# Mamba, attention and expert blocks on one core: expert weights split once and reloaded, shorter maximum and gate, and another order of steps between recurrences

## The reference

```
1  h = rmsnorm(x);  xi, z = split(h @ in_proj);  xi = silu(conv4(xi))
   dt, B, C = split(xi @ x_proj);  delta = softplus(dt @ dt_proj + b)
   s_t = s_(t-1) * exp(delta_t * A) + delta_t * B_t * xi_t        (16 states)
   y_t = sum_n s_t[n] * C_t[n];  x = ln(2x + ((y + D xi) * silu(z)) @ out_proj)
2  q with rotary positions, 8 heads, 128 keys of a fixed context
   x = ln(x + relu(ln(x + softmax(q k / sqrt(32)) v @ W_o) @ W_ffn))
3  top-2 of 8 experts by softmax(x @ gate), and one shared expert:
   x = ln(x + sum_e c_e * (silu(x @ w1_e + b1) * (x @ w3_e + b3)) @ w2_e)
```

## Time and profile before

| | |
|---|---|
| median of 3 runs | 1169.25 us (1169.08 to 1170.02) |
| the profiled execution | 1168.82 us, its span 1167.0 us |
| PE busy | 916.1 us (79%) |
| DVE busy | 828.9 us (71%) |
| ACT busy | 545.8 us (47%) |
| POOL busy | 535.4 us (46%) |
| granted TensorE clock, mean | 0.861 |
| DMA per expert besides w13s | w2s 256 KB, weight row (cbc) 256 KB; B (bbc) 512 KB for 4 steps |
| first recurrence (chunk 0 alone) | 61.8 to 160 us |
| recurrences of chunks 1, 2, 3 begin | 215.28, 478.05, 740.8 us |
| drain | from about 943 us |

### The profile page before, as it was taken

One profiled execution on the slowest core, in us unless ns is written; L12 is line 12 of the kernel. 1 busy time (PEld: TensorE's weight loads), 2 busy tenths in 40 slices (PEclk: granted clock), 3 DMA queues, 4 the chain that ended last, 5 costly groups with the idle time before them and its releaser, 6 DMA issues.

```text
span 1167.0 us, 13071 instructions
## 1 busy us (share of the span) xinstructions
PE 916.1 (79%) x4208; PEld 697.8 (60%) x4208; DVE 828.9 (71%) x1222; ACT 545.8 (47%) x1015; POOL 535.4 (46%) x318
## 2 busy tenths in 40 slices
PE   4857688486788998486788998477789985767996
PEld 2446673265677883265677883265678872645885
DVE  1699964698999954698999954698999961213233
ACT  3556736453455526453455526453555512413342
POOL 1267710743468720743468720743468723001552
PEclk9979999796689999796689999796689996755998
DMA  5111102101033302101033302102033212001330
GB/s 202 38 36 55 37 1 74 54 19 64 28 104 114 92 10 92 54 19 64 28 102 112 95 10 92 54 19 64 28 100 103 88 36 91 0 1 37 102 123 29
DMA packets 37714, 71.96 MB, mean 62 GB/s; under 512 B 3856, under 2 KB 12185, under 8 KB 37647
## 3 DMA queue, kind: packets, MB, share of 16 engines
q1 hardware_dynamic: 37646, 71.13, 18.9%
HBM read 64.62 MB, written 2.30 MB: 57 GB/s over the span
## 4 chain that ended last, share of the span: by engine, by line
PE 28%; issue 20%; POOL 19%; DVE 13%; ACT 5%; POOLq 0%; DMA 0%; DVEq 0%; ACTq 0%; SPq 0%
POOL dbu L537 11%; PE ps L928 8%; PE ps L1005 5%; DVE hs L1111 3%; POOL work L572 3%; PE ps L902 3%; PE ps L759 2%; DVE yacc L1164 2%; PE ps L848 2%; POOL w_lo L564 2%; DVE mx L1260 2%; POOL work L558 2%; POOL work L554 2%; PE ps L842 1%; ACT work L707 1%
## 5 line engine op out<-in xcount | busy, mean ns | idle before, releaser
L537 POOL TENSOR_TENSOR dbu<-v,bbc 128x1024 f32<-128x1024 f32 x128 | 301.8, 2364 | 218.0 <-DVE v L1097 124.4
L1111 DVE TENSOR_TENSOR_SCAN hs<-ps,carry,dbu 128x512 f32<-128x512 f32 x256 | 312.9, 1265 | 0.6 <-PE ps L759 0.6
L645 ACT ACTIVATE ps<-delta,neg_a 128x512 f32<-128x512 f32 x256 | 175.2, 691 | 174.0 <-DVE hs L1111 174.0
L759 PE MATMUL ps<-ident,hs 128*128 128x128 f32 x1024 | 161.2, 303 | 65.9 <-DVE yacc L1164 47.5
L759 PEld LDWEIGHTS ps<-ident,hs 128*128 128x128 f32 x1024 | 133.8, 158 | 90.5 <-DVE hs L1111 64.1
L564 POOL TENSOR_TENSOR w_lo<-w13s,w_hi 128x512 fp32r<-128x512 f32 x72 | 93.4, 1297 | 130.4 <-ACT w_hi L734 129.2
L1164 DVE SCALAR_TENSOR_TENSOR yacc<-ps,ctok,yacc 128x512 f32<-128x512 f32 x210 | 147.3, 737 | 1.9 <-PE ps L759 1.0
L1005 PE MATMUL ps<-w2s,work 128*128 128x256 f32 x576 | 136.3, 380 | 0.3
L747 ACT ACTIVATE work<-ps,half_b 128x512 f32<-128x512 f32 x72 | 49.6, 689 | 143.8 <-PE ps L928 139.8
L1005 PEld LDWEIGHTS ps<-w2s,work 128*128 128x128 f32 x576 | 105.8, 190 | 14.9 <-DVE work L1282 1.5
L928 PE MATMUL ps<-x_hi,w_hi 128*128 128x512 f32 x288 | 108.4, 458 | 7.6 <-DVE work L1282 7.3
(11 more groups left out here) (169 smaller groups left out, 1322.4 us busy)
## 6 DMA issues: line engine op xcount, KB each, us to landing
w13s<-in_w SPq DMA_DIRECT2D x72, 256.0 KB, 2.9
bbc<-brow_dram SPq DMA_DIRECT2D x32, 512.0 KB, 4.0
w2s<-in_w SPq DMA_DIRECT2D x36, 256.0 KB, 2.7
cbc<-comb_dram SPq DMA_DIRECT2D x32, 256.0 KB, 3.5
work<-work SPq DMA_DIRECT2D x16, 256.0 KB, 2.3
xn<-in_x SPq DMA_DIRECT2D x4, 512.0 KB, 4.7
xt<-in_x SPq DMA_DIRECT2D x4, 512.0 KB, 4.8
rope<-in_rope_q SPq DMA_DIRECT2D x4, 512.0 KB, 5.4
```

Source lines behind the costliest of these rows:

```text
L537: pool.tensor_tensor(dbu[:, i % DRING, :, :], v[:, 2 * h:2 * h + 2, :], bbc[:, n // 2 % 2, n % 2, :].rearrange("p (o t) -> p o t", o=1) .t ...
L645: act.activation(ps[:, unit % 2, :], delta[:, q, :], ACT.Exp, scale=neg_a[:, q * NS + m:q * NS + m + 1]).then_inc(da_done.sem, 1)
L759: last = pe.transpose(ps[:, bank, t * P:(t + 1) * P], src(t), ident[:, :])
L1111: dve.tensor_tensor_scan(hs[:, m % 2, q, 0:TC], ps[:, unit % 2, :], dbu[:, n % DRING, q % 2, :], carry[:, m, q:q + 1], ALU.mult, ALU.add). ...
```

## The change

It does four things.

1. **Weights split once.** During the recurrence of chunk 0 each of the 18 halves is loaded raw, split on ACT and POOL, and both parts are stored to DRAM (new step "split", at s = 2 to 20). Each chunk then loads both parts, twice 256 KB a half, into a ring of 4. The raw buffers share memory with xa and x2.
2. **Maximum.** 1/sqrt(32) is multiplied into the keys at set-up, DVE reduces with `negate=True` straight into `top`, and the scaling (L1263) goes.
3. **Gate.** gm becomes (b + b3) * gac, written over b in PSUM; hh becomes (th + 1) * gm with gm from PSUM. Both need b now.
4. **Order.** Step s stands with tick s + 3. Ticks 3 to 37 are inside the recurrence; ticks 0, 1 and 2 and what is left (38 to 40) stand between steps of "post" and "pre" as BETWEEN lists them. The q product now comes ahead of the delta product, the normalisation of x1 ahead of the convolution. x_proj uses PSUM bank 0 and the transposes of the rows bank 3, instead of 6 and 7.

```diff
-HRING = 3
+HRING = 4
-PRE_TICKS = 2
+PRE_TICKS = 3
+BETWEEN = ("post0", "post1", "left0", "left1", "post2", "pre1", "left2", "post3", "post4", "post5", "pre2", "left3", "pre3",
+           "tick0", "pre4", "tick1", "pre5", "tick2", "pre6")
...
-        steps += mixer(i, "pre", 1) + mixer(i - 1, "post", 3) + mixer(i - 1, "post", 4)
-        steps += mixer(i, "pre", 2) + mixer(i - 1, "post", 5) + mixer(i, "pre", 3)
-        steps += second(0)
-        steps += mixer(i, "pre", 4) + mixer(i, "pre", 5)
-        steps += second(1, ("early",)) + mixer(i, "pre", 6) + second(1, ("late",))
+        for what in BETWEEN:
+            kind, n = what[:-1], int(what[-1])
+            if kind == "left" and i >= 2:
+                steps += [("second", i - 2, p, PRE_TICKS + SCAN_TICKS + n) for p in ("early", "mid", "late")]
...
+            if i == 0 and 2 <= s < 3 + 2 * ALL:
+                steps += mixer(0, "split", s - 2)
...
-        for k, t in enumerate(range(PRE_TICKS + SCAN_TICKS, T_OUT + 1)):
-            if k < 3:
-                steps += mixer(i, "post", k)
-            steps += second(t)
...
+                if kind == "split":
+                    for c in range(4) if n == 0 else (n + 3,):
+                        if c < 2 * ALL:
+                            if c >= 4:
+                                sp.wait_ge(lo_done.sem, c - 3)
+                            sp.dma_start(w13s[c % 4].rearrange("p a n -> p (a n)"), w13[c]).then_inc(raw_in[c % 4].sem, 16)
+                    c = n - 1
+                    if c >= 0:
+                        sp.wait_ge(hi_done.sem, c + 1)
+                        sp.wait_ge(lo_done.sem, c + 1)
+                        for dst, src in ((hi_dram, w13_hi), (lo_dram, w13_lo)):
+                            sp.dma_start(dst[c], src[:, c % HRING, :, :, :].rearrange("p s k n -> p (s k n)")
+                                         ).then_inc(parts_out[c % HRING].sem, 16)
...
+                sp.wait_ge(*b_ps.at(j, max(0, c - HRING + 1)))
+                for dst, src in ((w13_hi, hi_dram), (w13_lo, lo_dram)):
+                    sp.dma_start(dst[:, c % HRING, :, :, :].rearrange("p s k n -> p (s k n)"), src[c]
+                                 ).then_inc(w13_in[c % HRING].sem, 16)
...
-                    act.wait_ge(*gm_done.at(j, max(0, c - 1)))
+                    act.wait_ge(*hh_done.at(j, max(0, c - 1)))
...
-                    pe.wait_ge(*lo_done.at(j, c + 1))
+                    pe.wait_ge(*w13_in[c % HRING].at(j, 32 * (c // HRING + 1)))
...
-                        dve.tensor_reduce(mx[:, :], s8, AX.X, ALU.max).then_inc(mx_done.sem, 1)
-                        dve.wait_ge(*mx_done.at(j, tile + 1))
                         dve.wait_ge(*p_done.at(j, tile))
-                        dve.tensor_scalar(top[:, :], mx[:, :], -HD ** -0.5, None, ALU.mult
-                                          ).then_inc(top_score_done.sem, 1)
+                        dve.tensor_reduce(top[:, :], s8, AX.X, ALU.max, negate=True).then_inc(top_score_done.sem, 1)
...
-                    dve.scalar_tensor_tensor(out=gm[:, ib, :], in0=th[:, ib, :], scalar=1.0,
+                    dve.wait_ge(*b_ps.at(j, c + 1))
+                    dve.scalar_tensor_tensor(out=ps[:, 5, :], in0=ps[:, 5, :], scalar=col("b3", c),
                                              in1=(gac if c >= 2 else ga)[:, ib, :],
                                              op0=ALU.add, op1=ALU.mult).then_inc(gm_done.sem, 1)
                     dve.wait_ge(*gm_done.at(j, c + 1))
-                    dve.wait_ge(*b_ps.at(j, c + 1))
+                    dve.wait_ge(*th_done.at(j, c + 1))
                     dve.wait_ge(*o_ps.at(j, max(0, c - 1)))
-                    dve.scalar_tensor_tensor(out=hh[:, ib, :], in0=ps[:, 5, :], scalar=col("b3", c),
-                                             in1=gm[:, ib, :], op0=ALU.add, op1=ALU.mult).then_inc(hh_done.sem, 1)
+                    dve.scalar_tensor_tensor(out=hh[:, ib, :], in0=th[:, ib, :], scalar=1.0,
+                                             in1=ps[:, 5, :], op0=ALU.add, op1=ALU.mult).then_inc(hh_done.sem, 1)
```

More of the change, by code:

```diff
@@ L86, in schedule @@
             steps += mixer(0, "setup", 0)
-        steps += mixer(i, "pre", 1) + mixer(i - 1, "post", 3) + mixer(i - 1, "post", 4)
-        steps += mixer(i, "pre", 2) + mixer(i - 1, "post", 5) + mixer(i, "pre", 3)
-        steps += second(0)
-        steps += mixer(i, "pre", 4) + mixer(i, "pre", 5)
-        steps += second(1, ("early",)) + mixer(i, "pre", 6) + second(1, ("late",))
+        for what in BETWEEN:
+            kind, n = what[:-1], int(what[-1])
+            if kind == "left" and i >= 2:
+                steps += [("second", i - 2, p, PRE_TICKS + SCAN_TICKS + n) for p in ("early", "mid", "late")]
+            if kind == "post":
+                steps += mixer(i - 1, "post", n)
+            if kind == "pre":
+                steps += mixer(i, "pre", n)
+            if kind == "tick":
+                steps += second(n)
         if i == 0:
             steps += mixer(0, "setup", 1)
+        if i == CHUNKS:
+            for t in range(PRE_TICKS, T_OUT + 1):
+                steps += second(t)
+            break
         for s in range(SCAN_TICKS):
@@ L355, in block_kernel @@
         cbc_in = [signal(f"cbc_in{s}", 16 * len(range(s, EXPERTS, CRING))) for s in range(CRING)]
-        w13_in = [signal(f"w13_in{s}", 16 * len(range(s, 2 * ALL, HRING))) for s in range(HRING)]
-        hi_done = signal("hi_done", 2 * ALL)
-        lo_done = signal("lo_done", 2 * ALL)
+        w13_in = [signal(f"w13_in{s}", 32 * len(range(s, 2 * ALL, HRING))) for s in range(HRING)]
+        raw_in, hi_done, lo_done = [one(f"raw_in{s}") for s in range(4)], one("hi_done"), one("lo_done")
+        parts_out = [one(f"parts_out{s}") for s in range(HRING)]
         w2_in = [signal(f"w2_in{s}", 16 * len(range(s, ALL, WRING))) for s in range(WRING)]
@@ L604, in mixer @@
                     normalise(j, "x1", x1, x1_done)
+                if kind == "split" and n < 2 * ALL:
+                    act.wait_ge(raw_in[n % 4].sem, 16 * (n // 4 + 1))
+                    if n >= HRING:
+                        act.wait_ge(parts_out[n % HRING].sem, 32 * (n // HRING))
+                    act.activation(flat_part(w13_hi, n), w13s[n % 4], ACT.Copy).then_inc(hi_done.sem, 1)
                 if kind == "pre" and n == 1:
@@ L809, in mixer @@
                         pe.wait_ge(*u_done.at(j, q + 1))
-                        last = pe.matmul(ps[:, 6, :], wxp[:, q, :], u[:, q, :], start=(q == 0), stop=(q == Q - 1))
+                        last = pe.matmul(ps[:, 0, :], wxp[:, q, :], u[:, q, :], start=(q == 0), stop=(q == Q - 1))
                     last.then_inc(xp_ps.sem, 1)
```

55 lines of the change are left out of this document (24 added, 31 removed).

## The result

Before 1169.63 us (median of 4 runs), after **1140.93 us** (4 runs, 1140.0 to 1141.65): ratio 0.9752, 95% interval 0.9737 to 0.9768. The gain is 28.7 us where 54 were forecast; the time lies outside the range of 1103 to 1137, on its slow side. The profiled execution has a span of 1138.2 us against 1167.0.

What follows compares the result with a forecast made beforehand. The bound was taken to change by stage: POOL's rotation, DVE with PE close behind, PE between recurrences, DVE in chunk 0. Terms 7 + 3 x (-15.4 + 0.4 - 4.8) + 2 x (-0.5) - 1 = -54.4 gave 1115 us, range 1103 to 1137.

Steps and rivals of the forecast that it cites:

- Splitting in chunk 0: First recurrence: 18 subtractions make POOL slower than DVE, partly hidden by run-ahead; +7 us once, bounds 3 and 23.
- Rival (e): Splitting costs its upper bound because POOL, ACT and the stores take turns: 1128 us, chance 0.05.
- Three equal recurrences: The sum counts start, expert ticks and chain behind alike for three recurrences: 3 x (-15.4 + 0.4 - 4.8) us.
- start: Start of a recurrence: DVE's stall of 8.27 us, the scalings and a pair of scans go; -15.4 us each.
- ticks: Expert ticks under the recurrence: PE sets the pace at 5.35 us, with one tick more inside; +0.4 us each.
- the chain behind: Behind the recurrence: DVE's chain to the output product replaces the tick that stood between; -4.8 us, three times.
- Rival (a): PE's clock falls in the preparation all the same, 3.8 us at each of three places: 1126 us, chance 0.15.
- Preparation: Between recurrences: PE without a hole at full clock, rotation ending near 473, scan at 477.5 against 478.05; -0.5 us, twice.
- signs of being wrong: Among them: a scan start later than 10 us after the last delta product, and POOL's rotation ending after v.
- Rival (b): Late rotation, swap or scores hold dbu or the second maximum, so half the stall stays: up to 1137 us, chance 0.12.
- Drain: After the last recurrence: PE's own pace, four scalings of about 0.25 us leave the chain; -1 us.
- (d): Rival: doubled weight loads come late and PE waits in each expert tick; 1210 us at 130 GB/s, chance 0.03.

Runs made afterwards that it cites:

- pool_late: The changed kernel, but in the recurrence of chunk 0 POOL subtracts one step after ACT has rounded: 1134.18 us.
- busy_pe: The changed kernel with unread products added on PE, 8 behind the delta product and 6 behind the first scores: 1126.6 us.
- b_late: The changed kernel, but SP issues the two broadcasts of B behind the swap of the q rows instead of ahead of it: 1125.21 us.
- resplit: The changed kernel, but weights are loaded raw and split again for every chunk as before the change: 1132.68 us.

## Why the prediction was wrong

**Splitting in chunk 0, "+7": too small by 7.7.** The rule behind it, 18 x 0.57 less POOL's run-ahead, was right for a POOL that never waits, and pool_late gives that (+8.2). The step that failed is the sentence "ACT's 18 roundings fit into its idle time": it looked at ACT's share and not at its order. ACT walks its list too, the rounding stands behind the exp of the same step, and POOL wants its result in that same step. Rival (e) named this ("take turns") at 0.05, for 13 us on top of the 7 (its own upper bound of 23 would make 16); 7.7 on top came. It deserved more, since every piece of the split was a hand-over between two engines in one step.

**Three equal recurrences, "3 x": wrong by 4.5 and 7.6.** Recurrence 1 came out within 0.5 us: start -16.2 (-15.4 forecast), ticks +0.7 (+0.4), the chain behind -4.8 (-4.8). The rows and the prediction told the second and third by the first. Two things differ:
- The last one of before was 3.3 us shorter already (205.0 against 208.3). PE's timeline of the kernel before, its product a of ticks 22 and 36 in recurrence 3:

```profile
859.30 0.73 PE L928 MATMUL ps<-x_hi,w_hi 128*128 128x512 f32 x2
...
935.81 0.81 PE L928 MATMUL ps<-x_hi,w_hi 128*128 128x512 f32 x2
```

  These 14 ticks took 76.5 us, not the 79.8 of recurrence 1, so PE lost 1.6 us to DVE there and not 4.9. The difference stands in two ticks. DVE's gm in the later of the two, in recurrence 1 and in recurrence 3:

```profile
372.81 2.79 DVE L1276 SCALAR_TENSOR_TENSOR work<-work 128x512 f32<-128x512 f32 x1
...
896.64 0.89 DVE L1276 SCALAR_TENSOR_TENSOR work<-work 128x512 f32<-128x512 f32 x1
```

  In the tick ahead of it gm lasts 2.80 and 1.66 us. The fetch of the next chunk has its instructions between them (L1064 on DVE at 368.98), and recurrence 3 has no next chunk to fetch; that this is the reason is argued from the rows, not tried. Where PE sets the pace that difference vanishes (193.0 and 192.9 after), so there was 3.3 us less to win.
- In recurrences 2 and 3 the clock falls a second and a third time in the steps ahead of the experts, 5.0 and 4.9 us against recurrence 1. Of these 5 us 2.4 are lost by the fourth maximum (32.75 us behind the first scan instead of 30.31), the rest by the first product a. Rival (a) had the fall cost 3.8 us in the products of the preparation; they ran at 1.00, and it came as the last of them ended and cost its time in the attention. The prediction looked at PE's clock up to the q product and stopped there ("no hole until the rotation").

The Trainium skill (page "TensorE: Matmul & The Clock Gate", section "What's actually happening") has the clock fall after an idle window and return after a busy one. The trace agrees that the clock stays low behind 8.40 us of idle PE (0.53) and comes back under the unread products (1.00 from 469 us on). It does not agree on every fall: in the changed kernel it came as the delta product ended, ahead of the idle time, and in busy_pe with PE busy for 3.60 of 3.60 us ahead of it. So the prediction's sentence that the trace shows a fall to follow idle time goes beyond its rows: in the kernel before, too, PE's last hole (0.69 us ahead of the row transposes) ended at 460.39, 3 us before the fall.

**Preparation, "-0.5": came out +1.7 and +1.9.** PE's part was right: from the start of the output product to the end of the delta product it was to be 467.3 - 430.45 = 36.9 us and is 461.80 - 425.05 = 36.8. The failed step is "The rotation ends near 473, before dbu is wanted; its cover is the delta product and softplus". That would be 5.7 us behind the delta product; it ended at 470.16, 8.4 behind it, beside v, which began at 466.56. The scan came 12.5 us behind the delta product instead of some 10. The prediction had both among its signs of being wrong. Rival (b) names it at 0.12; its place was v and the clock, not the second maximum. b_late shows why: the swap was costed by its place in PE's and POOL's order, and never against the megabyte that SP issues ahead of it; of SP's transfers only the weights were weighed.

**Drain, "-1": came +0.6.** The term took the four scalings for a part of the chain. From the first to the fourth maximum of the drain it is 27.1 us with them gone and was 27.2, so they were not. The drains of the twelve kernels lie between 218.8 and 225.8 us and go with the granted clock of their first 90 us: 0.84 in busy_pe (218.8), 0.76 in the changed kernel, 0.71 in resplit (225.8).

**Right:** the stall, ticks at PE's pace (5.37), gm at 0.76 whatever POOL does, weights hidden at 163 GB/s (so (d) falls), 7.6 us behind the recurrence. With POOL's wait, the rotation and the clock mended, and the weights split as before, the gain is 59.5 us of span: the amount forecast was there to be had, but in another kernel. That its size meets the forecast's 54 is partly luck: the busy PE, which no term of the forecast has, is in it.

What stays open: why recurrence 1 has no second fall of the clock, with a rotation as late as that of 2 and 3. The low clock comes and goes with shifts of a few microseconds, and no run here singles out what decides. Open too is what lets it fall with PE busy.

## What to carry to other kernels

Read an engine's order and not its busy share before you call its work hidden: a piece handed from one engine to another within the same step costs the receiver its run-ahead, and moving the receiver one step later won 6.5 us here and cost nothing. Two changes that take away the same cost are not worth their sum; price each with the other in place, and drop the one that has a price of its own. And where a stage is told once for several repetitions, compare their lengths first, and look at each transfer in front of a small urgent one on the same queue.
